# Six pairs of row scores one step later in the heads of an attention

## The reference

```
h    = layernorm(x) * (1 + ca) + sa
Q, K = h @ Wq.T, h @ Wk.T             # 8 heads of 64
V    = h @ Wv.T                       # 8 heads of 128
attn = softmax(einsum('bnhr,bmhr->bhnm', Q, K), axis=-1)
x    = x + ga * einsum('bhnm,bmhd->bnd', attn, V)
```

## Time and profile before

| what | value |
|---|---|
| median of 3 runs | 3081.31 us (3079.63 to 3084.49) |
| the profiled execution's own time | 3079.73 us |
| its span, first to last instruction | 3077.9 us |
| PE busy | 2810.5 us (91%) |
| DVE busy | 2286.6 us (74%) |
| ACT busy | 2189.3 us (71%) |
| POOL busy | 1779.8 us (58%) |

### The profile page before, as it was taken

How to read it: one execution, slowest core, us unless ns; L and a number is a source line. 1 busy time by engine, 2 the same in 40 slices (tenths; PEclk the granted TensorE clock), 3 DMA queues, 4 the chain that set the end, 5 groups by cost and what they waited for, 6 DMA issues and landing times. The chain is left out here.

```text
span 3077.9 us, 77592 instructions
## 1 busy us (share of the span) xinstructions
PE 2810.5 (91%) x27940; PEld 2083.9 (68%) x27940; DVE 2286.6 (74%) x8471; ACT 2189.3 (71%) x4273; POOL 1779.8 (58%) x1756
## 2 busy tenths in 40 slices
PE   5999999999999999999999995699998999898688
PEld 3777777777777777777777775466666666666443
DVE  6676776776766767767767645899999999997565
ACT  3888788788888887887887780565666666666575
POOL 3778777778778778778778781333333333332121
PEclk7999999999999999999999997687787787777799
DMA  3000000000000000000000001100000000000000
GB/s 102 1 1 8 1 1 8 1 1 8 1 1 8 1 1 8 1 1 8 1 1 8 1 1 63 66 0 0 0 0 0 0 0 0 0 0 2 8 21 28
DMA packets 11793, 27.63 MB, mean 9 GB/s; under 512 B 1529, under 2 KB 6137, under 8 KB 11137
## 3 DMA queue, kind: packets, MB, share of 16 engines
q1 hardware_dynamic: 11618, 25.48, 2.4%
HBM read 17.07 MB, written 8.40 MB: 8 GB/s over the span
## 5 line engine op out<-in xcount | busy, mean ns | idle before, releaser
L284 POOL TENSOR_TENSOR probs_l<-probs,probs_h 128x512 fp32r<-128x512 f32 x1024 | 1302.7, 1291 | 378.6 <-ACT probs_h L378 377.4
L377 ACT ACTIVATE probs<-bank 128x512 f32<-128x512 f32 x1024 | 625.8, 611 | 323.3 <-PE bank L698 297.0
L539 DVE TENSOR_REDUCE maxes<-ring 128x1 f32<-128x512 f32 x1024 | 659.0, 686 | 177.0 <-PE ring L678 176.2
L378 ACT ACTIVATE probs_h<-bank 128x512 fp32r<-128x512 f32 x1024 | 625.2, 611 | 0.0
L697 PE MATMUL bank<-q_hh,k_hl 128*128 128x512 f32 x1024 | 423.8, 414 | 0.2 <-ACT q_lm L367 0.2
L698 PE MATMUL bank<-q_lm,k_h 65*128 65x512 f32 x1024 | 405.1, 396 | 0.0
L708 PE MATMUL obank<-probs_h,x_l 128*128 128x512 f32 x1024 | 403.9, 394 | 0.0
L710 PE MATMUL obank<-probs_h,x_h 128*128 128x512 f32 x1024 | 402.8, 393 | 0.0
L709 PE MATMUL obank<-probs_l,x_h 128*128 128x512 f32 x1024 | 402.4, 393 | 0.0
L678 PE MATMUL ring<-k_hl,q_hh 128*128 128x512 f32 x1024 | 378.8, 430 | 24.5 <-DVE k_hl L523 6.0
L1074 ACT ACTIVATE low_hot<-obank 128x512 f16<-128x512 f32 x512 | 297.0, 604 | 66.7 <-PE obank L1249 53.6
(11 more groups left out here) (252 smaller groups left out, 4971.0 us busy)
## 6 DMA issues: line engine op xcount, KB each, us to landing
xt<-in_x SPq DMA_DIRECT2D x8, 512.0 KB, 10.2
out_x<-xt SPq DMA_DIRECT2D x8, 512.0 KB, 2.6
x<-out_x SPq DMA_DIRECT2D x1, 4096.0 KB, 12.2
out_x<-x SPq DMA_DIRECT2D x16, 256.0 KB, 2.1
mod<-out_x SPq DMA_DIRECT2D x3, 512.0 KB, 13.7
pk_wq<-in_w_q SPq DMA_DIRECT2D x1, 1024.0 KB, 4.8
pk_wqT<-in_w_qT SPq DMA_DIRECT2D x1, 1024.0 KB, 6.9
hot_rule<-in_hot_rule SPq DMA_DIRECT2D x1, 776.0 KB
```

Of the source, the lines that this page charges most:

```text
L284: nc.gpsimd.tensor_tensor(probs_l[:, i, :], probs[:, s % 4, :], probs_h[:, i, :].bitcast(F32), ALU.subtract).then_inc(low_ready, 1)
L377: nc.scalar.activation(probs[:, s % 4, :], st[s % 4], ACT.Exp)
L378: nc.scalar.activation(probs_h[:, i, :], st[s % 4], ACT.Exp).then_inc(st_free[s % 4], 1)
L539: nc.vector.tensor_reduce(maxes[:, i, k:k + 1], ring[bank_of(at)][:], AX.X, ALU.max).then_inc(rows_maxed, 1)
```

## The change

Two edits. `ROW_STEPS` goes from steps 3 to 8, 11 and 12 to steps 4 to 9, 11 and 12: the first six pairs of row scores of the next head are each made one step later. In DVE's `body` the maxima of a step are now written ahead of the additions of the output. It matters in step 9, which now has both: PE makes the row scores of a step before its outputs, and both use the same two banks in turn. The order of bank uses over a head is the same as before. PE's own program text is not edited; it reads `ROW_STEPS`.

```
-ROW_STEPS = (3, 4, 5, 6, 7, 8, 11, 12)
+ROW_STEPS = (4, 5, 6, 7, 8, 9, 11, 12)
...
                         if s == 1 and more and g:
                             q_and_k(b, h + 1)
-                        if s in (OUT_0, OUT_1) and g:
-                            gather_output(link, b - (h == 0), (h - 1) % H, int(s == OUT_1))
                         if s in ROW_STEPS and more:
                             row_maxima(b, h + 1, ROW_STEPS.index(s))
                             if s == ROW_STEPS[-1]:
                                 whole_max(b, h + 1)
+                        if s in (OUT_0, OUT_1) and g:
+                            gather_output(link, b - (h == 0), (h - 1) % H, int(s == OUT_1))
                         if s == MAXIMA and h == H - 2 and not last:
```

## The result

| | median us | range | runs |
|---|---|---|---|
| before | 3080.47 | 3074.36 to 3084.49 | 4 |
| changed | 3043.38 | 3021.76 to 3048.91 | 4 |

The ratio is 0.9861, 95% interval 0.9834 to 0.9888: the changed kernel is 1.4% faster, and the forecast, 3041, lies 2.4 us beside the median. The profiled execution has a span of 3040.8 us, 37.1 less than before; the sum had -39.0. The total is right, but of its three terms one is a sixth too large, one has the wrong sign, and the third is near only as the sum of unlike cases. The runs of the changed kernel also spread more, 27 us from lowest to highest.

The account below looks back on a forecast made before the run. The prediction took PE's instruction stream plus its waits to bound the kernel. -52.5 + 9.9 + 3.6 = -39.0 us against 3079.7 gave 3040.7; with the median 1.6 above it, the forecast was 3041, range 3028 to 3064.

Parts of the forecast that it names:

- three terms: Parts of the sum over 8 batches: heads 1 to 6 -52.5 us, head 0 +9.9, head 7 +3.6.
- The two waits: PE's waits in steps 3 and 4 of a head: 4.54 us in head 4, forecast 2.81 with no wait left.
- the 1.26 us: What steps 3 and 4 of head 4 wait together per head before the change: 4.54 us against 3.28.
- Heads 1 to 6 save 6.56 us a batch: Head 1 saves 0.91 us, heads 2 and 3 1.01 each, heads 4 to 6 1.21 each; 52.5 in 8 batches.
- between nothing and 0.2: Step 9: wait of its outputs for the bank, taken as 0.05 us, so 0.52 with the added pair.
- Other engines hide behind PE in ordinary heads: Heads 1 to 6: ACT costs nothing, POOL keeps some idle time, the join ends 0.87 us before PE needs it.
- C: Heads 1 to 6: POOL's slack is thinner, the join is passed over once, 0.44 us a head; 3062, chance 0.12.
- D: Heads 1 to 6: POOL never pauses and holds the join until index 14 is done; 3106, slower, chance 0.05.
- Head 0 is slower by 1.24: The join ends at 981.57 instead of 980.33, behind POOL's low parts: +1.24 us a batch, +9.9 in 8.
- rival E: DVE is held for one POOL instruction only: head 0 saves 2.1 us a batch, head 7 0.73; 3005, chance 0.04.
- Head 7 saves nothing and pays 0.52: L481 in step 3 is held by POOL's third low part, so nothing saved; step 9 costs 0.52, +3.6 in 7 batches.
- My rule for who gets in: POOL keeps going where its next operands were there long before; DVE gets in when POOL has nothing more.

Follow-up runs that it names:

- the one-input join: The changed kernel with the join of the maxima (L546) made by a one-input reduction instead of a two-input maximum: 3017.10 us, ratio 0.9791.
- the artificial late join: The changed kernel with the one-input join, plus four useless reductions ahead of it in head 0 of batches 2 to 8: 3045.15 us, ratio 0.9869.

## Why the prediction was right, point by point

- *The two waits are DVE's pace in steps 3 and 4, and go.* Shown: 2.87 us for the 2.81 forecast, and no wait of PE for the split or the additions is left. The additions still stand ahead of the first maxima, and cost PE nothing there now that the pair comes later. The kernel with the outputs in step 3 shows the other half: with the pair in step 3 and the additions behind it, the split alone holds PE for 0.92 us. How much of the 1.26 us the additions made is not shown by itself.
- *Heads 1 to 6 save 6.56 us a batch.* Mis-sized, by a sixth. Head 4 saves 27.54 - 26.51 = 1.03 instead of 1.21: 0.06 more in steps 3 and 4, 0.07 in step 5, 0.07 in step 9. I had called the pair of step 5 just in time, and the outputs of step 9 "between nothing and 0.2". A matmul whose bank came free just in time stopped PE for some 0.1 us here. Over the eight batches the starts of the scores give 0.70, 0.83, 0.98, 1.00, 1.02 and 0.99 for heads 1 to 6: 5.5 us a batch, 44 us for the 52.5 of the sum.
- *Other engines hide behind PE in ordinary heads.* Right. The join is 1.1 us there, head 4 is 26.51 with it and 26.50 with the one-input join: rivals C and D did not come.
- *Head 0 is slower by 1.24, DVE gets in when GpSimd runs dry.* Half right. In five of seven batches the join ended just where the forecast put it, 26.9 us into the head, but the head took 31.5 and not 30.0. (PE came 0.7 us earlier to its wait and not 1.0: 23.9 us into the head, 24.6 before.) What failed is that a wait was priced at its own length: the clock falls behind 3.1 us of standing and takes 1.5 us more. In two of seven DVE got in at the first boundary, and the head took 26.7, 2.05 less than before: rival E, which had 2.1 and a chance of 0.04. The term came to +10.7 in this profile against +9.9, but as the sum of unlike cases, of which none is 1.24: -2.05 in two batches, +2.7 to +3.7 in five, and nothing in the first.
- *Head 7 saves nothing and pays 0.52.* Wrong. It takes 27.58 instead of 28.21. The step that failed is "the third is ready by then, so DVE is held". DVE asked at the forecast time, 6.5 us into the head, and the third low part was ready: its exponential ended at 1130.69, 0.7 us before it began. DVE got in all the same at the end of the second, in all seven batches of this profile:

```profile
1128.90 3.96 POOL L284 TENSOR_TENSOR probs_l<-probs,probs_h 128x512 fp32r<-128x512 f32 x3 [3.38 <-ACT probs_h L378]
1130.55 1.18 DVE L481 TENSOR_TENSOR wv_gated<-wv_sb,mod 128x256 f32<-128x256 f32 x1
1131.65 1.96 DVE L539 TENSOR_REDUCE maxes<-ring 128x1 f32<-128x512 f32 x3
```

  The seven batches win 4.4 us where the sum had 3.6 lost. It is rival E's head 7, which had 0.73 a batch and 5 in all.
- *The sum.* -44 + 10.7 - 4.4 = -38 against a span 37.1 us shorter. In the first term 8.5 us too much was forecast as won, in the last 8 too little, and the two errors cancelled. That the total was right to 2.4 us is partly luck, and so is any single run of this kernel, given its spread.
- *My rule for who gets in* (GpSimd wins a boundary where it has had its next operands for long) did not stand. GpSimd's operands were 2 us old at the boundary where the fifth batch's join got in. Operands 0.7 us old kept the join out in the kernel before, but did not keep L481 out in head 7. What decides is open: the same program gives both with the same times up to that boundary, so it isn't the order of instructions, nor the moment of asking to within 0.02 us. That DVE can wait past several boundaries, the profiles of all kernels with the two-input join show. In none of them did it wait longer than GpSimd's run.

## What to carry to other kernels

A product can be made one step later when its reader is late for it: here that won 1.67 us and cost 0.66 in each ordinary head. Look then for the next place where the same reader meets two jobs in neighbouring steps, because a pair just behind the additions made the same wait anew. A two-input instruction of VectorE that the next engine waits for, beside a GpSimd that never pauses, was a lottery in this kernel. Give it one input where that is possible: here a reduction over 16 numbers did the same work. A long wait of TensorE, here 2.6 and 3.1 us, is to be priced with the slower clock behind it (about 1.5 us here), and a bank that comes free just in time with about 0.1 us, as in steps 5 and 9 here.

## What the runs showed of the hardware

- A two-input VectorE instruction waited until up to five instructions of GpSimd in a row were done (5.17 us for 0.42 with L481, 5.16 for 0.17 with the join). The same join in the same batch got in at the first boundary in another execution (0.24 us). The Trainium skill, SBUF — State Buffer, "Who interferes with whom", has the shared pair as an exclusive lock that whoever issues first gets for the whole instruction; the short cases agree (0.24 us), while in the long ones VectorE had asked before four of the five GpSimd instructions began. It also says that `tensor_reduce` never contends on this chip: the trace agrees, 64 of 64 at 0.17 us.
- Behind a wait of TensorE of 2.6 us the granted clock was 0.55 for 3.5 us, and behind one of 3.1 us for 3.6 us. Behind the 1.1 us of the kernel before the next 3.6 us ran at 1.00 (window below), and so did the 3.5 us behind one of seven waits of 2.6 us with the artificial late join. That the clock follows how busy TensorE was is in the Trainium skill, TensorE: Matmul & The Clock Gate, "Part 1: The HAM clock gate (the "warmup" mystery)"; these windows agree, and nothing measured here tells why one of the seven equal waits had no fall behind it.

```profile
980.40:984.00 3.60, 3.60 (x22) 3.03 (x23) 2.40 (x17) 3.09 (x6) 1.97 (x2) 1.00 0.02 5
```
